# A pair's first product ahead of the unit's gate, routing pieces between a unit's operations, own places for the last rows

## What is computed

```
mod = silu(c) @ wmod                 -> sa, ca, ga, sb, cb, gb per batch; |ga|, |gb| at least 0.25
h   = layernorm(x) * (1 + ca) + sa
x   = x + ga * mix(h)                # token shift, three products, exp and sigmoid, output product,
                                     # then the channel mix with three more products
h   = layernorm(x) * (1 + cb) + sb
shared = (silu(h Wsg') * (h Wsu')) Wsd'          # 704 hidden, for every row
scores = softmax(h Wr'), the best two of 8 experts
routed = sum over the two: score * (silu(h Wg') * (h Wu')) Wd'   # 352 hidden
x   = x + gb * (shared + routed)
```

## Time and profile before

| | |
|---|---|
| device time, three runs | 1936.57, 1941.3, 1943.7 us; median 1941.3 |
| profiled execution | 1946.47 us, its span 1944.7 us |
| TensorE busy | 1754.3 us, 90% of the span |
| VectorE busy | 1345.7 us, 69% |
| ScalarE busy | 767.5 us, 39% |
| GpSimd busy | 556.6 us, 29% |
| mean granted TensorE clock | 0.945 |
| channel stage's end to first expert unit | about 1076 to 1148 us |
| LATE part | about 1680 to 1940 us |

### The profile page before, as it was taken

How to read it: one execution, slowest core, us unless ns; L and a number is a source line. 1 busy time by engine, 2 the same in 40 slices (tenths; PEclk the granted TensorE clock), 3 DMA queues, 4 the chain that set the end, 5 groups by cost and what they waited for, 6 DMA issues and landing times.

```text
span 1944.7 us, 28391 instructions
## 1 busy us (share of the span) xinstructions
PE 1754.3 (90%) x9093; PEld 1522.8 (78%) x9093; DVE 1345.7 (69%) x2468; ACT 767.5 (39%) x1147; POOL 556.6 (29%) x631
## 2 busy tenths in 40 slices
PE   4599999996769999999989879999999999977778
PEld 0488888885558878878878779999999999866678
DVE  4899999983687877777775436666766766544442
ACT  2333333342335545545543124545545554321211
POOL 0344444431444435545545300000000000144410
PEclk8799999998889999999999889999999999987879
DMA  8422222213423434545546777777677776555421
GB/s 325 150 92 90 87 89 88 86 65 110 141 101 138 147 137 171 191 161 187 191 158 220 240 278 250 256 273 249 239 270 255 261 261 237 166 167 159 151 86 44
DMA packets 141350, 338.78 MB, mean 174 GB/s; under 512 B 20632, under 2 KB 20632, under 8 KB 135760
## 3 DMA queue, kind: packets, MB, share of 16 engines
q1 hardware_dynamic: 110576, 250.15, 37.7%
q10 hardware_dynamic: 20448, 54.01, 7.4%
q0 software_dynamic: 10240, 33.56, 4.9%
HBM read 230.14 MB, written 107.53 MB: 174 GB/s over the span
## 4 chain that ended last, share of the span: by engine, by line
PE 66%; DVE 19%; issue 5%; ACT 4%; DMA 3%; POOL 2%; SPq 1%; DVEq 0%; ACTq 0%; POOLq 0%
PE bank L566 17%; PE bank L567 16%; PE bank L568 16%; DVE mix L1547 5%; PE bank L577 4%; PE bank L2042 3%; PE bank L2040 3%; PE bank L2041 3%; PE bank L2035 2%; DVE xm_lo L1553 1%; ACT xm_hi L1150 1%; DVE raw L1869 1%; DVE hid L1631 1%; POOL diff L1003 1%; ACT raw L1345 1%
## 5 line engine op out<-in xcount | busy, mean ns | idle before, releaser
L566 PE MATMUL bank<-gu_hi,ex_x_hl 128*128 128x352 f32 x1136 | 395.0, 348 | 4.3 <-DMA ex_x_hl<-h_turned 2.4
L567 PE MATMUL bank<-gu_lo,ex_x_hl 128*128 128x352 f32 x1136 | 381.1, 335 | 0.0
L568 PE MATMUL bank<-gu_hi,ex_x_hl 128*128 128x352 f32 x1136 | 380.2, 335 | 0.0
L1084 POOL DMA_INDIRECT raw<-expert_out_rows,out_slots x64 | 83.0, 1296 | 659.4 <-DMA expert_out_rows<-y_rows 569.8
L566 PEld LDWEIGHTS bank<-gu_hi,ex_x_hl 128*128 128x128 f32 x1136 | 227.7, 200 | 4.8 <-DMA ex_x_hl<-h_turned 2.7
L567 PEld LDWEIGHTS bank<-gu_lo,ex_x_hl 128*128 128x128 f32 x1136 | 227.2, 200 | 0.0
L568 PEld LDWEIGHTS bank<-gu_hi,ex_x_hl 128*128 128x128 f32 x1136 | 226.0, 199 | 0.0
L1631 DVE TENSOR_TENSOR hid<-bank,sg_t 128x352 f32<-128x352 f32 x142 | 73.9, 521 | 214.0 <-ACT sg_t L1208 211.2
L1547 DVE SCALAR_TENSOR_TENSOR mix<-diff,vecs,h2T 128x128 f32<-128x128 f32 x256 | 160.6, 695 | 80.5 <-POOL diff L1003 80.5
L1208 ACT ACTIVATE sg_t<-bank 128x352 f32<-128x352 f32 x142 | 66.1, 466 | 332.0 <-PE bank L568 331.7
L2040 PE MATMUL bank<-dn_hi,hid_hi 128*128 128x512 f32 x426 | 170.2, 400 | 8.3 <-DVE hid_lo L1635 8.3
(11 more groups left out here) (229 smaller groups left out, 4028.4 us busy)
## 6 DMA issues: line engine op xcount, KB each, us to landing
raw<-in_ex_gu SPq DMA_DIRECT2D x39, 1408.0 KB, 6.8
raw<-in_ex_dn SPq DMA_DIRECT2D x39, 512.0 KB, 7.5
ex_x<-expert_in_rows SPq DMA_DIRECT2D x78, 256.0 KB, 2.9
expert_out_rows<-y_rows ACTq DMA_DIRECT2D x78, 256.0 KB, 4.1
h_rows<-h_t SPq DMA_DIRECT2D x64, 256.0 KB, 2.4
h_turned<-h_hl ACTq DMA_DIRECT2D x32, 512.0 KB
ex_x_hl<-h_turned ACTq DMA_DIRECT2D x32, 512.0 KB
x_t<-in_x SPq DMA_DIRECT2D x32, 256.0 KB, 2.6
```

Of the source, the lines that this page charges most:

```text
L566: pe.matmul(acc, act_hi[i], w_hi[i], start=(i == 0), stop=False)
L567: pe.matmul(acc, act_hi[i], w_lo[i], start=False, stop=False)
L568: last = pe.matmul(acc, act_lo[i], w_hi[i], start=False, stop=(i == chunks - 1))
L1084: pool.indirect_dma_start(rows[:, pair % 2, a, :], None, ys_d, bass.IndirectOffsetOnAxis(ap=out_slots[:, k, n:n + 1], axis=0)).then_inc(ar ...
```

## The change

Three things. `first_product` of a pair now stands between `hid_hi` and `sg_t` in ScalarE's list. Of the routing pieces, `softmax_and_first`, `second`, the first 13 operations of `tile_tables` (now `expert_tables`) and `result_slots` now stand between `hid_lo` and `hid` in their unit; `row_slots` and the rest of `tile_tables` stay behind. And the rows of tiles 26 to 29 get places of their own in `base`, which is still free then; tiles 30 and 31 use `sc_rows` once tiles 24 and 25 are scattered; the loads of tiles 24 to 29 move ahead of `mod3`'s.

```diff
+        def last_rows(n):
+            return base[:, n - 26, :] if n < 30 else sc_rows[:, n % 2, :]
...
+            def load_last_scattered(n):
+                sp.dma_start(last_rows(n), h3_d[n * P:(n + 1) * P, :]).then_inc(sc_last_in[n // 30], 16)
             wait_a2(sp)
+            for n in range(24, 26):
+                load_scattered(n)
+            for n in range(26, 30):
+                load_last_scattered(n)
             sp.wait_ge(raw_pad, 2)
             ...                                    # mod3's four loads
-            for n in range(24, 26):
-                load_scattered(n)
             for n in range(FU, FU + 2):
                 load_residual(n)
             sp.wait_ge(*base_vec.done(FU - 1, "base"))
             sp.dma_start(xres_d[(FU - 1) * P:FU * P, :], rs_t[:]).then_inc(rs_out, 16)
             for n in range(FU + 2, SPLIT):
                 load_residual(n)
-            for n in range(26, NT):
-                load_scattered(n)
+            for n in range(30, NT):
+                sp.wait_ge(sc_out[n % 2], 32 * 13)
+                load_last_scattered(n)
             sp.wait_ge(route_done, 1)
...
-                sp.wait_ge(sc_out[p], 32 * (NT // 2))
+                sp.wait_ge(sc_out[p], 32 * 13)
+            sp.wait_ge(sc_last_out, 32 * (NT - 26))
...                                                 # GpSimd
-            for n in range(24, NT):
+            def scatter_last(n):
+                pool.wait_ge(route_vec, (group_of(n) + 1) * ROUTE_OPS)
+                pool.wait_ge(sc_last_in[n // 30], 64 if n < 30 else 32)
+                for k in range(2):
+                    pool.indirect_dma_start(xs_d, bass.IndirectOffsetOnAxis(ap=slots[:, k, n:n + 1], axis=0),
+                                            last_rows(n), None).then_inc(sc_last_out, 16)
+            for n in range(24, 26):
                 scatter(n)
+            for n in range(26, NT):
+                scatter_last(n)
...                                                 # ScalarE, LATE
                     hidhi_before(*LATE.before(t, half))
+                    for q in range(NT // 2):
+                        if combined_at(q) == (n, half):
+                            first_product(q)
                     silu(LATE.unit(t, half), bank_of(LATE, half))
                     ...
-                    for q in range(NT // 2):
-                        if combined_at(q) == (n, half):
-                            first_product(q)
...                                                 # VectorE, EARLY
-            ROUTING = {0: (softmax_and_first, second), 1: (row_slots,), 2: (tile_tables,), 3: (result_slots,)}
+            BEFORE_HID = {0: (softmax_and_first, second), 2: (expert_tables,), 3: (result_slots,)}
+            AFTER_HID = {1: (row_slots,), 2: (tile_tables,)}
...
                     hidlo(*EARLY.before(t, half))
+                    pieces(BEFORE_HID, t, half)
                     if t.only(SPLIT - 1) and half:
                         expert_lo(FIRST, 0)
                     hid_of(EARLY, t, half)
                     ...                            # the base, in the first half
-                    for piece in ROUTING.get(2 * (t.n - FU) + half, ()):
-                        piece(*([] if piece in (tile_tables, result_slots) else [LAST]))
+                    pieces(AFTER_HID, t, half)
```

More of the change, by code:

```diff
@@ L465, in build @@
         sc_out = pair_of_sems("sc_out")
+        sc_last_in = pair_of_sems("sc_last_in")
+        sc_last_out = sem("sc_last_out")
         pad_out = sem("pad_out")
@@ L1744, in _, with expert_tables @@
                 dve.memset(raw[i][F % P:P, RAW - D:RAW], 0.0).then_inc(raw_pad, 1)
-            def tile_tables():
+            def expert_tables():
                 total, padded, end, end2 = (count[name] for name in ("total", "padded", "end", "end2"))
@@ L1760, in tile_tables @@
                 link(dve.tensor_scalar(step[:], padded[:], -1.0, float(REGION), ALU.mult, ALU.add))
+            def tile_tables():
+                cur = count["end" if E.bit_length() % 2 else "end2"]
                 dve.wait_ge(table_const, 1)
@@ L1783, in _, with pieces @@
             LAST = len(GROUPS) - 1
-            ROUTING = {0: (softmax_and_first, second), 1: (row_slots,), 2: (tile_tables,), 3: (result_slots,)}
+            BEFORE_HID = {0: (softmax_and_first, second), 2: (expert_tables,), 3: (result_slots,)}
+            AFTER_HID = {1: (row_slots,), 2: (tile_tables,)}
+            def pieces(table, t, half):
+                for piece in table.get(2 * (t.n - FU) + half, ()):
+                    piece(*([LAST] if piece in (softmax_and_first, second, row_slots) else []))
             def hid_of(part, t, half):
```

## The result

The changed kernel takes 1854.6 us (median of four, 1854.1 to 1859.9), the kernel before 1941.5 (four, 1936.6 to 1943.7): ratio 0.9562, 95% interval 0.9537 to 0.9587, so 87 us faster. I had said 1848, within 1838 to 1870. The profiled execution took 1854.4 us, its span is 1852.7 us, the mean granted clock 0.968 (before 0.945).

A forecast was written before the change was run, and what follows sets the result against it. TensorE, 90% busy, was taken as the bound, plus its waits and lower clock. Late units 83.1 and passage 10.5 made 93.6 us off 1946.47: 1852.9, less 5.2 to the median: 1847.7, said as 1848; range 1838 to 1870.

The forecast's parts named there:

- Part 1: Late combining units: first product ahead of the gate's Silu removes TensorE's 16 waits for `hid`, 83.1 us gained.
- The products' margin: ScalarE, late units: the copy to `out` lands at T+13 (T: unit's start), needed at T+12.77+1.1 to 1.5.
- rival 4: ScalarE, late units: late `cb_y1` or copy to `out` stops `sg_t`; 1953 at a 21 us landing; 2%.
- my sign of being wrong: Turns over 7 us apart, ScalarE waiting for `raw` ahead of `sg_t`, or a `hid_lo` wait before 1147 over 4 us.
- Rival 1: Combining units: VectorE or GpSimd becomes the bound, 7.25 us a unit, 14 us more, 1862; 20%.
- Rival 3: Combining units: each gather also stops VectorE 0.95 us, 9.4 us a unit, 48 us more, 1896; 4%.
- Part 2: Passage: routing pieces moved between a unit's VectorE operations, tables ready at 1105.5; 0.7 to 3.8 us, not added itself.
- Part 3: Passage: own places for the last rows free SyncE; expert's load 11.1 us earlier, passage gains 10.5 us, bounds 5 to 14.
- `mod3`'s landing: Passage: `mod3`'s four loads, issued till about 1087, land at 1091 (range 1090 to 1097), at no cost to TensorE.
- Passage: The stretch into the routed experts: 9.5 to 11.1 us gained, taken as 10.5.
- Rival 2: Passage gives little: `mod3` late or clock lost at each short wait, 5 us instead of 10.5, 1853; 10%.
- 5.2 us of offset: Whole kernel: the profiled execution before stood 5.2 us above the median 1941.3, so 1852.9 became 1847.7.

The follow-up runs named there:

- experiment 1: Also `p1_alone`: the kernel before with only the pair's first product moved ahead of Silu in ScalarE's list; 1864.2 us, ratio 0.960.
- experiment 7: The kernel before with only VectorE's late list changed, `hid` made ahead of the pair's weighted sum; 1874.9 us, ratio 0.9655.
- Experiment 8: Also `one_more_copy`: the changed kernel with an extra unused 0.62 us ScalarE copy ahead of each pair's products; 1855.0 us, ratio 0.9563.
- Experiment 6: The changed kernel with the last rows' loads and scatters (tiles 24 to 31) as before and `mod3`'s loads ahead again; 1864.2 us, ratio 0.9594.
- experiment 5: Also `without_p2`: the changed kernel with all routing pieces behind each unit's last VectorE operation again; 1860.0 us, ratio 0.9586.
- expert2_early: Also 9: the changed kernel with the second expert's weights issued ahead of the first expert rows' loads; 1855.2 us, ratio 0.9559.
- split_sum: The changed kernel with the gated multiplications of the weighted sum moved behind `hid` in VectorE's late list; 1853.8 us, ratio 0.955.
- experiment 2: Also `p23_alone`: the changed kernel with the first product put back behind Silu, its other changes kept; 1932.5 us, ratio 0.9953.
- experiments 3: Also `mod3_first`: the changed kernel with `mod3`'s four loads back ahead of the six loads of scattered rows; 1856.8 us, ratio 0.9576.
- 4: Also `mod3_wait_late`: the changed kernel with VectorE waiting for `mod3` a tile later, where it first reads it; 1855.7 us, ratio 0.9561.
- 10: The changed kernel with VectorE's `mod3` wait later and the second expert's weights issued earlier; 1851.3 us, ratio 0.9538.
- 12: The changed kernel with the later `mod3` wait, the earlier second expert's weights and the gated multiplications behind `hid`; 1849.7 us, ratio 0.9537.

## Why the prediction was right, and where it was off

**Part 1: right in mechanism and size.** The LATE units were put at 6.38 us each and took 6.42; 83.1 us were forecast, 82.5 came. The eight short waits of 0.2 to 0.3 us for the second unit of a tile are there as a pace (6.45 us against 6.26 in most tiles), though most are too short to be listed. The three that are listed have another cause, the copy to `out`, which is next. The pair of units takes 12.72 us, forecast 12.77. These are traces; by the medians of experiment 1 the part is worth 78.0. Experiment 1 shows that this part does it; experiment 7 shows that it was right to ask for the whole list of VectorE and not for `hid` alone.

**The products' margin** was smaller than I put it. I followed the copy to `out` to T+13 against a need at T+12.77+1.1 to 1.5. Five of the 16 pairs' products waited for it, 0.22, 0.42, 1.44, 0.79 and 0.54 us, since the copy took 4.3 us in the median (before 3.8). The longest is on ScalarE:

```profile
1738.69 0.20 ACT L1365 ACTIVATE act_col<-eps 128x1 f32<-128x1 f32 x1 [1.44 <-DMA out<-raw]
```

It puts the sum at 1740.23 and `hid` at 1742.82, and TensorE waits the 0.91 us at 1743.49. The waits of 0.79 and 0.54 stand in the units that end with TensorE's listed waits of 0.25 and 0.26. These three units took 7.31, 6.65 and 6.64 us where the other second units take 6.45 or 6.46: 1.25 us together. It is rival 4's late copy in small, and nearly my sign of being wrong (ScalarE waiting for `raw` ahead of `sg_t`), but what came late was the sum and not `sg_t`, which was still made 4.4 us after the turn. Experiment 8 shows that half a microsecond more of ScalarE's work in that place costs nothing.

**Rival 1** (7.25 us a unit) didn't happen. Gathers took 1.17 us in the mean, some of them 1.62 as the earlier trace rows had it, and GpSimd kept pace.

**Rival 3, the lock of both sides,** is refuted: no operation of VectorE took longer beside a gather. The base addition at 1699.01 took 0.69 us with gathers on both sides of it, and the last section has one that began inside a gather. Gathers alone were slowed, those that began inside an operation. The Trainium skill, SBUF — State Buffer, section Who interferes with whom, has the whole block on both sides, by issue order; these rows show it on one side only, GpSimd's.

**Part 2: its step failed, its sum not.** I priced the pieces by themselves and left them out of the sum, "as the next part ends later". Experiment 6 confirms that for the kernel without part 3 (0 us). Its two waits came nearly as forecast, 0.92 us (about 1) and 1.10 (1.5). But together with part 3, experiment 5 shows about 5 us: the pieces ahead of `hid` run while VectorE is not yet stopped by `mod3`.

**Part 3: the mis-sized term is `mod3`'s landing.** I took 1091 out of 1090 to 1097, and cost it at nothing as TensorE wanted `hid_lo` at about 1092. It landed at 1093.6 (`expert2_early` 1093.95, `without_p2` 1094.4, `split_sum` 1095.85), and TensorE lost 3.76 us in the changed kernel, 6.39, 7.59 and 9.26 in three others (`expert2_early`, `one_more_copy`, `split_sum`) which came there earlier. The landing holds the end, whenever TensorE arrives: its down products start at 1094.34, 1094.66, 1096.44 and 1096.55. The loads were issued by 1085.2, earlier than the 1087 that I had; it is the time from issue to landing that was wrong. I took it from the expert rows (2.7 us), and the trace of before had it for these very loads. Landing of `mod3`, median us, before and changed:

```profile
mod<-mod_rows SPq DMA_DIRECT2D x4, 256.0 KB, 6.1
mod<-mod_rows SPq DMA_DIRECT2D x4, 256.0 KB, 7.2
```

The slowest of the four took 9.0 us in the changed kernel, 7.9 before. Issue till 1087 and 6.1 to 7.9 would have said 1093 to 1095, and a wait of TensorE of 1 to 3 us. With the landing late, SyncE's expert load went out at 1110.87, forecast 1106.6. The step from there to the expert rows was 22.1 us instead of the 24.2 that I kept, which gave 2 us back. Passage: forecast 10.5, measured 7.8 in the traces, 9.7 by the medians of experiment 2. Rival 2 (5 us) had the right mechanism, `mod3`, and too high a price.

**What was not in any step: 5.2 us of offset.** Trace against trace I forecast 1852.9 and the profiled execution took 1854.4, 1.5 off. I then took off 5.2, because the profiled execution of before lay that far above its median. But executions of before vary with the clock that they are granted (1934.1 us at 0.953, 1946.5 at 0.945), and the profiled one was among the longest; the changed kernel's lies at its own median. Of 93.6 forecast, 92.1 came between the two profiled executions and 86.9 between the medians. My correction was right in kind only if the excess lay in time that the change leaves; it went with the change's stretch or with chance, and these runs don't say which. The one other trace that keeps the 16 waits (`p23_alone`) has 182.4 us for the 16 units against 182.64, but it too is a long execution, 3.8 above its median. The offset is the larger part of the 6.6 us that I was off.

**What stays open:** why a semaphore of TensorE seems to come 2 to 8 us late around 1094 to 1109 in experiments 3, 4, 10 and 12. DMA was at full share there each time, with scatters, loads and the store at once. But in the changed kernel the same share (1.01 from 1092 to 1104) goes with no such delay, TensorE waiting for `mod3` at that time. The same thing happens in LATE: in `p1_alone` the `hid_hi` of the first combining unit starts at 1702.30, 2.80 us after its turn instead of 0.58, at a DMA share of 0.88 (1699.5 to 1702.5), and TensorE then waits 1.59 us for `hid`. In `expert2_early` and `mod3_wait_late` it costs 1.6 and 1.5 us at the same unit, so two traces can differ by that much for no reason in their edits. I have not shown the DMA to be the cause.

## To carry to other kernels

When an in-order engine does side work between two things that the bound engine waits for, look for the wait in that engine's own list that is there anyway, and put the side work into it; then follow the next engine's whole list, as curing only the wait that the profile names (experiment 7) moved a seventh of the gain into the next one. A load that is moved behind others is late by the time that their issues take and by its own landing, which is to be read from its own row and not from that of another load of its size. When a passage is held by several landings in a row, removing one may show nothing until the next is moved too (by medians 4 and 9 gave nothing, and 10 was 3.9 us under 9). Compare trace with trace and median with median: how far one profiled execution lies from its median did not carry over here.

## What the runs showed of the hardware

Between a gather and a VectorE operation with two inputs in SBUF, only the gather ever paid in the changed kernel, and only when it began second. Timeline of GpSimd in the changed kernel: the gather of 1696.16 began inside the operation of 1695.73 and took 1.61 us, ending 0.8 us behind the end of that operation. (The row of before that I read as 0.95 behind gives 0.8 too: 1709.59 + 1.62 against 1709.15 + 1.22.) The gather of 1729.20 took its 0.96 us.

```profile
1696.16 1.61 POOL L1107 DMA_INDIRECT raw<-expert_out_rows,out_slots  x1 [0.30 <-issue]
1698.08 0.95 POOL L1107 DMA_INDIRECT raw<-expert_out_rows,out_slots  x1 [0.30 <-issue]
...
1729.20 0.96 POOL L1107 DMA_INDIRECT raw<-expert_out_rows,out_slots  x1 [0.30 <-issue]
```

Timeline of VectorE: this addition began inside that last gather, and took the 1.22 us that all of its kind take (13 of them, 1.215 to 1.226; the 16 of L1906 take 1.224 to 1.226).

```profile
1729.68 1.22 DVE L1919 TENSOR_TENSOR raw<-raw,base 128x1024 f32<-128x1024 f32 x1
```

The four `mod3` loads, 256 KB each, take 5.9 to 9.0 us from issue to landing in the changed kernel, behind six others. Ahead of those six they take 4.9 to 7.8 in `mod3_first` and 5.1 to 7.9 in the kernel before. So being behind them adds about 1 us to the landing itself; 5.5 of the 6.35 us between the ends of VectorE's waits (1087.28 and 1093.63) are the later issue (first one at 1077.70 and 1083.22). The six loads of rows in front of them in the changed kernel, 256 KB each too, land in 3.0 and 4.1 us in the median (two into `sc_rows`, four into `base`). What makes the `mod3` loads slower than these is not shown: they also differ in form, one row written to all 128 partitions.
